# A recurrent stage with attention: batch halves half a step apart, token gates made beforehand in fp32, and one power for two groups in the slot stage

## What is computed

```python
x_in = _ln(x, lnkv_g, lnkv_b)
k = x_in @ wk + bk
v = x_in @ wv + bv
slots = q_mu + jnp.exp(q_logsig) * noise
for _ in range(T):
    prev = slots
    q = _ln(slots, lnq_g, lnq_b) @ wq + bq
    logits = jnp.einsum('bnd,bkd->bnk', k, q) / scale        # scale = D ** -0.5
    attn = jax.nn.softmax(logits, axis=-1) + EPS_ATTN
    attn = attn / jnp.sum(attn, axis=1, keepdims=True)
    upd = jnp.einsum('bnk,bnd->bkd', attn, v)
    slots = upd @ wu + bu + prev
    h = _ln(slots, lnm_g, lnm_b) @ w1 + b1
    slots = jax.nn.gelu(h, approximate=False) @ w2 + b2 + slots
    slots = _ln(slots + x_cls[:, None, :], lnp_g, lnp_b)
```

```python
def step(h, x_t):
    proj = h @ W
    score = jnp.einsum('bsh,bh->bs', enc_hiddens, proj)
    attn = jax.nn.softmax(score, axis=-1)
    context = jnp.einsum('bs,bsh->bh', attn, enc_hiddens)
    inp = jnp.concatenate([x_t, context], axis=-1)
    gx = inp @ kernel + bias
    gh = h @ recurrent_kernel
    xz, xr, xh = (gx[:, :Hd], gx[:, Hd:2 * Hd], gx[:, 2 * Hd:])
    hz, hr, hh = (gh[:, :Hd], gh[:, Hd:2 * Hd], gh[:, 2 * Hd:])
    z = jax.nn.sigmoid(xz + hz)
    r = jax.nn.sigmoid(xr + hr)
    cand = jnp.tanh(xh + r * hh)
    h_new = z * h + (1.0 - z) * cand
    return (h_new, h_new)
```

## Time and profile before

| | before |
|---|---|
| median of 3 executions | 9187.53 us (9184.92 to 9192.29) |
| the profiled execution | 9142.96 us, span 9141.2 us |
| busy share of PE, DVE, ACT, POOL | 72%, 57%, 32%, 9% |
| mean granted TensorE clock | 0.786 |

### The profile page before, as it was taken

The page is one execution under the profiler, slowest core; times in us unless marked ns, Lnnn a source line. Parts: engine busy times, 40 slices in busy tenths (PEclk is TensorE's granted clock), DMA queues, the critical chain, the costliest instruction groups (busy, mean ns, idle before and its releaser), DMA issues. The chain is left out here.

```text
span 9141.2 us, 219716 instructions
## 1 busy us (share of the span) xinstructions
PE 6593.8 (72%) x93385; PEld 4903.5 (54%) x93385; DVE 5207.4 (57%) x18123; ACT 2915.1 (32%) x5070; POOL 791.1 (9%) x776
## 2 busy tenths in 40 slices
PE   3442226778787664888888788788888888888875
PEld 2331114556565333777777565465555656565553
DVE  5555664444444666555555434775757576675752
ACT  1221112233332221111111111454545555454541
POOL 1112320000000000000000000111111011111100
PEclk7666557889888785555555798899999998999996
DMA  1000000000000000000000000000000000000000
GB/s 28 0 0 2 0 0 24 1 1 1 1 1 2 2 0 4 4 4 4 4 4 4 20 0 4 12 2 9 2 9 2 6 5 2 9 2 9 2 4 9
DMA packets 61268, 45.65 MB, mean 5 GB/s; under 512 B 22521, under 2 KB 56126, under 8 KB 60228
## 3 DMA queue, kind: packets, MB, share of 16 engines
q1 hardware_dynamic: 60355, 32.26, 1.3%
HBM read 30.14 MB, written 2.10 MB: 4 GB/s over the span
## 5 line engine op out<-in xcount | busy, mean ns | idle before, releaser
L366 DVE TENSOR_REDUCE peak<-ps 128x8 f32<-128x1024 f32 (+1 forms) x832 | 816.5, 1023 | 270.9 <-PE ps L288 270.2
L408 ACT ACTIVATE e<-ps,H_lowT_c 77x1024 f32<-77x1024 f32 x384 | 405.1, 1104 | 266.4 <-PE ps L312 266.4
L408 ACT ACTIVATE e<-ps,H_lowT_s 128x1024 f32<-128x1024 f32 x384 | 406.7, 1110 | 249.8 <-PE ps L312 249.8
L135 POOL TENSOR_TENSOR rstd<-veps,neghalf 128x4 f32<-128x4 f32 x80 | 80.5, 1006 | 4496.0 <-DVE veps L126 4496.0
L326 PEld LDWEIGHTS ps<-e,H_vt 128*32 128x32 f32 (+1 forms) x12288 | 323.8, 113 | 259.1 <-ACT e L408 143.2
L326 PE MATMUL ps<-e,H_vt 128*32 128x128 f32 (+1 forms) x12288 | 438.9, 284 | 23.6 <-DVE xs L386 17.7
L142 PE MATMUL ps<-ident,zn 128*128 128x128 f32 x256 | 71.3, 434 | 519.7 <-DVE zn L129 519.7
L312 PE MATMUL ps<-H_qr,H_km 32*128 32x128 f32 (+1 forms) x12288 | 430.8, 279 | 0.0
L312 PEld LDWEIGHTS ps<-H_qr,H_km 32*128 32x128 f32 (+1 forms) x12288 | 416.3, 173 | 16.2 <-issue 3.0
L1556 PE MATMUL ps<-F_hp,F_encW 128*128 128x3 bf16 (+2 forms) x12288 | 367.3, 166 | 64.2 <-DVE F_hp L1482 63.8
L1556 PEld LDWEIGHTS ps<-F_hp,F_encW 128*128 128x128 bf16 x12288 | 347.2, 104 | 85.0 <-DVE F_hp L1482 84.5
(11 more groups left out here) (593 smaller groups left out, 14951.0 us busy)
## 6 DMA issues: line engine op xcount, KB each, us to landing
G_w<-in_L_ffn_w SPq DMA_DIRECT2D x16, 256.0 KB
H_f<-in_L_xcond_f_w SPq DMA_DIRECT2D x12, 256.0 KB
H_nw<-in_L_xcond_n_w SPq DMA_DIRECT2D x21, 128.0 KB, 2.1
A_cond<-in_cond SPq DMA_DIRECT2D x1, 2048.0 KB
out_x<-x_all SPq DMA_DIRECT2D x1, 2048.0 KB, 8.7
ctx_rows<-in_ctx SPq DMA_DIRECT2D x1, 1232.0 KB
D_wq<-in_L_xcond_attn_wq SPq DMA_DIRECT2D x2, 512.0 KB
D_wk<-in_L_xcond_attn_wk SPq DMA_DIRECT2D x2, 512.0 KB
```

The source lines that it names most:

```text
L366: last = nc.vector.tensor_reduce(peak[:, HL * half:HL * (half + 1)], view, AX.X, ALU.max, negate=True)
L408: nc.scalar.activation(e[0:keys, half, :], ps[0:keys, AGAIN[half]:AGAIN[half] + 2, :].rearrange("p b t -> p (b t)"), ACT.Exp, bias=low(u) ...
```

## The change

In the recurrent stage the two halves are half a step apart: PE, DVE and ACT go through `k` = 0 to 31 half-steps (half `k % 2` of step `k // 2`), and in one turn of the loop half `k` does its scores and softmax while half `k - 1` makes its context's parts, its gates and its state. Each part of a split has its own signal, and score and gate products are ordered by the part that they read. The token's share of the gates is made ahead of the loop for all tokens with 24 fp32 products (`F_tok`), and enters the gates through one fp32 product with the identity, of 48 columns, in place of 18 bf16 products. The work ahead of the loop is one block, with the contexts' parts on POOL and the moves on ACT. In the slot stage there is one power of 128x8 for both groups, in 7 of 12 normalisations ACT scales the second group, and the softmax's subtraction and sum are done within 4 exponentials per group.

```diff
-        for j in range(2):
-            nc.vector.tensor_scalar(vepss[j][0:rows], mvs[j][0:rows, :, 1], LN_EPS, None, ALU.add).then_inc(sem["var_ready"], 1)
-        for j in range(2):
-            dve.wait_ge(sem["rstd_ready"], at(r, j))
+        nc.vector.tensor_scalar(veps2[0:rows], mv2[0:rows, :, :, 1], LN_EPS, None, ALU.add).then_inc(sem["var_ready"], 1)
+        dve.wait_ge(sem["rstd_ready"], r + 1)
+        if shared:
+            nc.vector.scalar_tensor_tensor(out=drop[0:rows], in0=mv2[0:rows, 1, :, 0], scalar=-1.0, in1=rstd2[0:rows, 1, :],
+                                           op0=ALU.mult, op1=ALU.mult).then_inc(sem["drop_ready"], 1)
+        for j in range(1 if shared else 2):
...
-            step(nc.vector.tensor_reduce(am[:], per(bank(j, 2))[0:CL], AX.X, ALU.max))
-            nc.vector.tensor_tensor(attn[:], per(bank(j, 2))[0:CL], am[:].unsqueeze(2).broadcast_to([CL, U, S]),
-                                    ALU.subtract).then_inc(sem["shifted"], 1)
+            step(nc.vector.tensor_reduce(am[:], per(bank(j, 2))[0:CL], AX.X, ALU.max, negate=True))
+            nc.vector.tensor_scalar(am[:], am[:], float(D) ** 0.5, None, ALU.mult).then_inc(sem["shifted"], 1)
-            step(nc.vector.tensor_reduce(ar[:], attn[:], AX.X, ALU.add))
             step(nc.vector.reciprocal(ar[:], ar[:]))
-            step(nc.vector.tensor_tensor(attn[:], attn[:], ar[:].unsqueeze(2).broadcast_to([CL, U, S]), ALU.mult))
-            nc.vector.tensor_scalar(attn[:], attn[:], 1e-8, None, ALU.add).then_inc(sem["upd_ready"], 1)
+            for u in range(U):
+                last = nc.vector.tensor_scalar(attn[:, u, :], attn[:, u, :], ar[:, u:u + 1], 1e-8, ALU.mult, ALU.add)
+            last.then_inc(sem["upd_ready"], 1)
...
-            nc.gpsimd.tensor_tensor(rstds[j][0:rows], vepss[j][0:rows], neghalf[0:rows, 0:U],
-                                    ALU.pow).then_inc(sem["rstd_ready"], 1)
...
                                     scale=col[scale][:] if scale else 1.0)
+    def normalise(k, src, rows=128):
+
+        act.wait_ge(sem["drop_ready"], k + 1)
+        for u in range(U):
+            last = nc.scalar.activation(zns[1][0:rows, u, 0:D], src(u), ACT.Identity, bias=drop[0:rows, u:u + 1],
...
         for j in range(2):
             act.wait_ge(sem["shifted"], at(it, j))
-            nc.scalar.activation(attns[j][:], attns[j][:], ACT.Exp, scale=float(D) ** 0.5).then_inc(sem["exp_done"], 1)
+            for u in range(U):
+                last = nc.scalar.activation(attns[j][:, u, :], per(bank(j, 2))[0:CL, u, :], ACT.Exp, bias=ams[j][:, u:u + 1],
+                                            scale=float(D) ** 0.5, accum_out=ars[j][:, u:u + 1])
...
+        nc.gpsimd.memset(encW[:, :, :, CL:128], 0.0)
+        pool.wait_ge(sem["var_ready"], 1)
+        nc.gpsimd.tensor_tensor(rstd_b[:], veps_b[:], neghalf[:, 0:B], ALU.pow).then_inc(sem["rstd_ready"], 1)
+        for g in range(NG):
+            mine = slice(g * U, (g + 1) * U)
+            rest_ = xs[0:CL]
+            step(nc.gpsimd.tensor_copy(ctxp[:, 0, mine, :], ctx_tm[:, mine, :]))
+            step(nc.gpsimd.tensor_tensor(rest_, ctx_tm[:, mine, :], ctxp[:, 0, mine, :], ALU.subtract))
+            step(nc.gpsimd.tensor_copy(ctxp[:, 1, mine, :], rest_))
+            step(nc.gpsimd.tensor_tensor(ctxp[:, 2, mine, :], rest_, ctxp[:, 1, mine, :], ALU.subtract))
...
+            if g + 1 < NG:
+                turn(g + 1)
+            pe.wait_ge(sem["xnT_ready"], g + 1)
+            for i in range(3):
+                q = 3 * g + i
+                if q >= 4:
+                    pe.wait_ge(sem["proj_read"], q - 3)
+                nc.tensor.matmul(ps[:, 4 + q % 4, :], gate_w["x"][:, i * D:(i + 1) * D], zzT[:, g % 2, :],
+                                 start=True, stop=True).then_inc(sem["proj_done"], 1)
...
+    def score(k):
+        t, c = k // CH, k % CH
+        for i, made in ((2, "h_high"), (1, "h_middle"), (0, "h_low")):
+            if t > 0:
+                pe.wait_ge(sem[made], k - 1)
+            for j in range(CB):
+                b = CB * c + j
+                last = nc.tensor.matmul(scored(k)[:, 3 * j:3 * j + 3 - i], encW[:, i, b, :], hp[:, b, 0:3 - i],
+                                        start=(i == 2 and j == 0), stop=(i == 0), skip_group_check=True)
+        last.then_inc(sem["scores_done"], 1)
...
+            pe.wait_ge(sem["x_ready"], 1)
+        if t == EARLY and c == 0:
+            pe.wait_ge(sem["later_ready"], 1)
+        nc.tensor.matmul(ps[:, 4 * c + 3, 0:3 * CB].rearrange("p (i b) -> p i b", i=3), ident[:], xloc[:, t, :, mine(c)],
+                         start=True, stop=False, skip_group_check=True)
...
+    def late(k):
+        c = k % CH
+        for b, made in ((0, "c_high"), (1, "c_middle"), (2, "c_low")):
+            pe.wait_ge(sem[made], k + 1)
+            for a in range(3 - b):
+                for i in range(3):
+                    last = nc.tensor.matmul(gate(k, i), gate_p["c"][:, a, i * D:(i + 1) * D], cvp[:, c, :, b],
+                                            start=False, stop=(b == 2), skip_group_check=True)
+        last.then_inc(sem["gate_done"], 1)
...
+    for k in range(HALVES):
+        score(k)
+        of_token(k)
+        of_state(k, PRODUCTS[0:3])
+        turn_scores(k)
+        if k > 0:
+            late(k - 1)
+        turn_weights(k)
+        of_state(k, PRODUCTS[3:6])
+        attend(k)
+    late(HALVES - 1)
...
+    def attended(k):
+        c = k % CH
+        dve.wait_ge(sem["pv_done"], k + 1)
+        step(nc.vector.tensor_reduce(t1[:, c, :], attended_bank(k)[:, 0:2 * CB].rearrange("p (j i) -> p j i", i=2), AX.X, ALU.add))
+        nc.vector.tensor_tensor(cvp[:, c, :, 0], t1[:, c, :], den[:, c, :], ALU.mult).then_inc(sem["c_high"], 1)
+        step(nc.vector.tensor_tensor(cv[:, c, :], t1[:, c, :], den[:, c, :], ALU.mult))
+        nc.vector.tensor_tensor(left[:, c, :], cv[:, c, :], cvp[:, c, :, 0], ALU.subtract)
+        nc.vector.tensor_tensor(cvp[:, c, :, 1], cv[:, c, :], cvp[:, c, :, 0], ALU.subtract).then_inc(sem["c_middle"], 1)
+        dve.wait_ge(sem["c_middle"], k + 1)
+        nc.vector.tensor_tensor(cvp[:, c, :, 2], left[:, c, :], cvp[:, c, :, 1], ALU.subtract).then_inc(sem["c_low"], 1)
...
+    def state(k):
+        t, c = k // CH, k % CH
+        new = hist[:, t + 1, mine(c)]
+        part = lambda i: hp[:, mine(c), i]
+        dve.wait_ge(sem["hid_ready"], k + 1)
+        step(nc.vector.tensor_tensor(t1[:, c, :], zh[:, c, :], cand[:, c, :], ALU.mult))
+        nc.vector.scalar_tensor_tensor(out=part(0), in0=keep[:, c, :], scalar=0.5, in1=t1[:, c, :],
+                                       op0=ALU.mult, op1=ALU.subtract).then_inc(sem["h_high"], 1)
+        step(nc.vector.scalar_tensor_tensor(out=new, in0=keep[:, c, :], scalar=0.5, in1=t1[:, c, :],
+                                            op0=ALU.mult, op1=ALU.subtract))
+        nc.vector.tensor_tensor(left[:, c, :], new, part(0), ALU.subtract)
+        nc.vector.tensor_tensor(part(1), new, part(0), ALU.subtract).then_inc(sem["h_middle"], 1)
+        dve.wait_ge(sem["h_middle"], k + 1)
...
+    for k in range(HALVES + 1):
+        if k > 0:
+            attended(k - 1)
+        if k < HALVES:
+            scores(k)
+            maximum(k)
+            turned(k)
+        if k > 0:
+            candidate(k - 1)
+            blend(k - 1)
+            state(k - 1)
+        if k < HALVES:
+            denominators(k)
...
-    for t in range(RUN):
-        for part in (score, turn_scores):
-            for c in range(CH):
-                part(t, c)
-        for c in range(CH):
-            of_state(t, c)
-            turn_weights(t, c)
-        for part in (attend, late):
-            for c in range(CH):
-                part(t, c)
-        if t + 1 < RUN:
-            for c in range(CH):
-                of_token(t + 1, c)
-
...
-    for t in range(RUN):
-        for part in (scores, maximum, turned, attended):
-            for c in range(CH):
-                part(t, c)
-        for c in range(CH):
-            candidate(t, c)
-            blend(t, c)
-            state(t, c)
```

More of the change, by code:

```diff
@@ L1492, in _ @@
                         step = Steps(dve, sem["vector_step"])
+                        for b in range(B):
+                            last = nc.vector.bn_stats(stats_b[:, b, :], x_all[:, b, :])
+                        step(last)
+                        for b in range(B):
+                            last = nc.vector.bn_aggr(mv_b[:, b, :], stats_b[:, b, :])
+                        step(last)
+                        nc.vector.tensor_scalar(veps_b[:], mv_b[:, :, 1], LN_EPS, None, ALU.add).then_inc(sem["var_ready"], 1)
@@ L1509, in _, with keys, turn @@
                     @block.tensor
                     def _(pe):
+                        def keys(g):
+                            if g >= 2:
+                                pe.wait_ge(sem["k_read"], g - 1)
```

(30 more changed lines are left out.)

313 lines of the change are left out of this document (150 added, 163 removed).

## The result

| | before | after |
|---|---|---|
| median | 9186.23 us (4 runs, 9107.66 to 9192.29) | 8921.74 us (4 runs, 8909.99 to 8937.1) |
| ratio | | 0.9732, 95% interval 0.9677 to 0.9788 |
| span of the profiled execution | 9141.2 us | 8910.1 us |

The median before differs from the one given above because a fourth execution was added (9107.66).

What follows compares the result with a forecast made beforehand. It took the order of waits as the bound, neither engine being full. Terms -170, -66 and +20 make -216 on the profiled 9143, 8927; with 44.6 added for the median 8972, stated as 8970, range 8915 to 9045.

Steps and rivals of the forecast that it cites:

- Recurrent loop, -170: Main loop: shifting the halves gives half-steps of 4.97 us and a body of 168.0 instead of 189.2, saving 170 us.
- VectorE binds by 0.07: Loop half-step: TensorE is ready for the scores' transpose at 3.54 us, VectorE's scores only at 3.61 with the hand-over.
- The 0.21: Loop, fp32 identity product: two weight loads of 107 ns by the skill, leaving TensorE 0.3 to spare; the forecast used 0.46.
- B: Rival, loop: the clock rises above 0.50 with TensorE 90% busy, saving 77 us more, 8895; chance 8%.
- A: Rival, loop: partial overlap, TensorE late at each transpose, half-step 5.3 us, saving 85 instead of 170, 9055; chance 12%.
- C: Rival, loop: TensorE's weight-and-product pairs cost more when halves alternate, 0.038 us instead of 0.027, giving 9220; chance 4%.
- D: Rival: the slot stage loses all it may, +35 us, and the block ahead of the loop gains only 48, 9005; 7%.
- E: Rival, loop: semaphore order undoes the shift and halves fall back into step, leaving only the token products' saving, 9080; 3%.
- Ahead of the loop, -66: Work before the recurrent loop: one block with four engines takes 56 us instead of 122.4, saving 66 (48 to 72).
- VectorE's own splits lie under that: Block ahead of the loop: VectorE's splits (encW, then c and h) are hidden under GpSimd's chain, which ends near 48 us.
- Slot stage, +20: Slot stage: the common power and ScalarE scaling cost 31 us, the new softmax gives 11, net +20 (+5 to +35).
- The addition of 44.6 us: Whole kernel: the runs' median, 9187.5, lay 44.6 us above the profiled execution, so this was added to 8927, giving 8972.

Runs made afterwards that it cites:

- e1: The changed kernel with both halves put back in the same phase, everything else kept: span 9041.7 us, body 184.4 us against 168.2.
- e7: The changed kernel with TensorE's transpose of the scores moved ahead of the first nine state products: loop 1321.3 us against 1341.9.
- e2: The changed kernel with a second fp32 identity product of 48 columns per half-step, into unread columns: body 181.5 us against 168.2.
- e5: The changed kernel with VectorE's main-loop operations reordered to fill its waits, the work itself the same: loop 1326.9 us against 1341.9.
- e6: The changed kernel with both the VectorE order of e5 and the TensorE order of e7: loop 1267.5 us against 1341.9.

## Why the prediction was right, and where it was not

- *Recurrent loop, -170.* Measured -167.1. The walk along VectorE's order held: 4.92 summed, 4.88 measured, by parts 0.86 for attended (0.92), 0.65 for scores to maximum (0.59), and the rest within 0.02 of its term. That the shift gives it, and not the lighter token products, is what e1 showed: 16.2 of 21.0 us a body. That the body came out at 168.2 for 168.0 is luck, two small errors that cancel: the half-step is 0.09 shorter than taken, and a body has 11.9 us beside its 32 half-steps where I counted 9.0.
- *"VectorE binds by 0.07."* This step was wrong in sign. In the changed kernel the transpose of the scores starts 0.32 to 0.33 after the scores' sum (4155.47, 4155.80), in e7 0.25: TensorE was late by about 0.07 there. The rows of e7 (timeline):

```profile
4153.95 0.20 DVE L1703 TENSOR_REDUCE F_sT<-ps 77x16 f32<-77x48 f32 x1
...
4154.20 0.30 PE L1652 MATMUL ps<-ident,F_sT 77*16 77x77 f32 x1
```

  e2 shows no slack on TensorE, e5 and e7 that neither engine binds alone. The sum survived since the two chains lay so close that either gives 4.9. The 0.21 that the forecast worked out from the Trainium skill ("TensorE: Matmul & The Clock Gate", LDWEIGHTS) with two weight loads, which would have given TensorE 0.3 of slack, is not borne out for the fp32 identity product: it holds TensorE for 0.44, near the 0.46 of the row with 8 columns. Whether the rule or the count of two loads fails was not tried.
- *The rivals.* B: the clock stayed at 0.50 with TensorE 90% busy, and 94% busy in e6. A: the half-step is 4.88 and not 5.3. C: 48 pairs still take 1.44 us, 0.027 each (4158.66). D: the slot stage lost 16 and not 35. E: with the halves in step (e1) a body is 184.4 and not 168.2.
- *Ahead of the loop, -66.* Measured -61.7, but by another path than forecast. GpSimd's chain ended at 3509.56, 45 us after the block's start, near the 48 forecast, but it was not what the loop waited for. "VectorE's own splits lie under that" was wrong: the 24 normalisations beside GpSimd took 0.98 us on average, the last 8 took 0.34, and VectorE set the pace of a group, with TensorE waiting 2.11 for it (3498.79). TensorE did find the fast clock. The forecast 56 us were a choice between 50 and 70 for TensorE alone, so that 60.7 came out near them is in part luck.
- *Slot stage, +20.* Measured +16.0, near the forecast by luck, since it is made of terms of another size: the power 128x8 is 1.637 us for 1.64 and costs 28.1 for the 31 of all rounds; the scaling on ScalarE, taken as even, costs 11.6 (1.65 against 1.11 per group in the rows, 0.41 per round in the stage); the softmax, taken at -11, gives 23.7. That last one was mis-sized by staying between two rows; the estimate that the forecast drew from the Trainium skill ("ScalarE: Activation LUTs", What ACT_TABLE_LOAD costs) for an activation with a pointer bias, 0.29, was nearer (-23), though with the accumulator read one follows the other after 0.34.
- *The addition of 44.6 us* between the profiled execution and the median is the main reason why the forecast was 48 high: in the changed kernel the profiled execution (8911.95) and the median (8921.74) lie only 10 apart, which makes 35 of the 48. The sum for the changed stages was right to 3 us (-216 against -212.8, with errors of +3, +4 and -4 in its parts); the rest is what the unchanged stages did by themselves. The addition had no mechanism behind it.
